# A pair-interaction tower on one core: later units become the moving rows, thirty rounds are added before they are summed

## The reference, cut to what matters

```python
e = jnp.stack([tbl_f[ids[:, f]] for f in range(40)], axis=1)    # 512 x 40 x 64
viW = jnp.einsum('bpd,pde->bpe', e[:, i_idx, :], W)             # all 780 pairs i < j
z = jnp.einsum('bpe,bpe->bp', viW, e[:, j_idx, :])              # 512 x 780
h = jnp.maximum(jnp.concatenate([z, dense_ctx], 1) @ W_top1 + b_top1, 0.0)
h = jnp.maximum(h @ W_top2 + b_top2, 0.0)
y = h @ W_top3
```

## Time and profile before

| | |
|---|---|
| median of 3 runs | 315.83 us (315.57 to 318.13) |
| profiled execution | 316.28 us, of which 314.0 us are the span of its instructions |
| PE busy | 307.4 us (98%) |
| DVE busy | 255.2 us (81%) |
| ACT busy | 135.6 us (43%) |
| POOL busy | 193.2 us (62%) |

### The profile page before, as it was taken

One profiled execution on the slowest core, in us unless ns is written; L12 is line 12 of the kernel. 1 busy time (PEld: TensorE's weight loads), 2 busy tenths in 40 slices (PEclk: granted clock), 3 DMA queues, 4 the chain that ended last, 5 costly groups with the idle time before them and its releaser, 6 DMA issues.

```text
span 314.0 us, 4400 instructions
## 1 busy us (share of the span) xinstructions
PE 307.4 (98%) x1676; PEld 112.0 (36%) x1676; DVE 255.2 (81%) x262; ACT 135.6 (43%) x338; POOL 193.2 (62%) x156
## 2 busy tenths in 40 slices
PE   7999999999999999999999999999999999999996
PEld 2444233333333323333333333333333333333464
DVE  4992999889898888989989999999999999950000
ACT  0497874875539545659974602066000000001032
POOL 3887777777777777777733887746665555650000
PEclk9999999999999999999999999999999999999999
DMA  5936232323223743232325689886779664440000
GB/s 147 316 113 206 66 92 62 93 61 79 74 62 94 277 149 91 58 92 64 92 54 118 142 192 179 166 191 153 167 167 188 139 135 92 94 83 8 10 0 0
DMA packets 16188, 35.87 MB, mean 114 GB/s; under 512 B 3748, under 2 KB 4776, under 8 KB 14504
## 3 DMA queue, kind: packets, MB, share of 16 engines
q0 software_dynamic: 5824, 16.79, 27.6%
q1 hardware_dynamic: 8264, 14.20, 15.1%
q10 hardware_dynamic: 2080, 4.61, 4.2%
HBM read 22.87 MB, written 0.00 MB: 73 GB/s over the span
## 4 chain that ended last, share of the span: by engine, by line
PE 63%; POOL 24%; issue 8%; DMA 3%; DVE 0%; ACT 0%; ACTq 0%
PE y_ps L671 39%; POOL gathered L338 24%; PE z_ps L695 14%; PE y_ps L705 5%; PE t_ps L705 2%; DMA gathered<-in_tbl,ids_sb 2%; PE y_ps L759 2%; DMA ids_sb<-ids_rows 1%; PE t_ps L759 1%; DVE prod L559 0%; PE y_ps L768 0%; ACT prod L472 0%; ACTq L368 0%; ACT y_out L475 0%; DVE x_fold L527 0%
## 5 line engine op out<-in xcount | busy, mean ns | idle before, releaser
L671 PE MATMUL y_ps<-x,w 64*128 64x512 f32 x780 | 182.8, 604 | 0.9 <-DVE prod L559 0.8
L338 POOL DMA_INDIRECT gathered<-in_tbl,ids_sb x128 | 127.6, 997 | 43.4 <-issue 38.4
L559 DVE TENSOR_TENSOR prod<-y_ps,x 128x1024 f32<-128x1024 f32 x89 | 103.8, 1210 | 15.3 <-PE y_ps L671 14.4
L559 DVE TENSOR_TENSOR prod<-y_ps,x_quad 128x1024 f32<-128x1024 f32 x96 | 110.4, 1214 | 1.3 <-issue 0.6
L671 PEld LDWEIGHTS y_ps<-x,w 64*128 64x128 f32 x780 | 70.2, 186 | 113.4 <-issue 81.3
L410 ACT COPY x<-x_fold 32x128 f32<-32x128 f32 x240 | 70.9, 295 | 68.4 <-DVE x_fold L527 65.7
L363 POOL TENSOR_TENSOR prod<-prod 128x2048 f32<-128x2048 f32 x12 | 54.5, 4540 | 33.2 <-DVE prod L559 33.2
L695 PE MATMUL z_ps<-prod,select 128*32 128x512 f32 x588 | 73.4, 600 | 0.0
L439 ACT COPY zT<-z_ps 128x512 f32<-128x512 f32 x6 | 3.5, 586 | 69.7 <-PE z_ps L695 69.7
L695 PEld LDWEIGHTS z_ps<-prod,select 128*32 128x32 f32 x588 | 14.3, 108 | 52.0 <-issue 36.8
L433 ACT COPY x_mix<-x 64x512 f32<-64x512 f32 x40 | 24.7, 617 | 0.7
(11 more groups left out here) (46 smaller groups left out, 89.1 us busy)
## 6 DMA issues: line engine op xcount, KB each, us to landing
w<-w_rows SPq DMA_DIRECT2D x48, 256.0 KB, 2.8
prod<-prod POOLq DMA_DIRECT2D x12, 1024.0 KB, 7.7
gathered<-in_tbl,ids_sb POOLq DMA_INDIRECT x128, 2.5
w<-w_rows ACTq DMA_DIRECT2D x1, 1792.0 KB, 8.2
prod<-in_tbl ACTq DMA_DIRECT2D x6, 256.0 KB, 7.8
prod<-hot_ids SPq DMA_DIRECT2D x4, 256.0 KB, 6.7
prod<-in_tbl ACTq DMA_DIRECT2D x4, 128.0 KB, 3.0
w<-w_rows ACTq DMA_DIRECT2D x1, 512.0 KB, 9.8
```

Source lines behind the costliest of these rows:

```text
L338: nc.gpsimd.indirect_dma_start(gathered[:, slot, c, s * DIM:(s + 1) * DIM], None, tables[f][:, :], bass.IndirectOffsetOnAxis(ap=ids_sb[:, ...
L559: nc.vector.tensor_tensor(prod[:, d % PROD_SLOTS, :, :], y_ps[:, d % DUO_SLOTS, :, :], factor, ALU.mult).then_inc(prod_ready, 1)
L671: last = nc.tensor.matmul(y_ps[:, d % DUO_SLOTS, half, :], w[rows, r % W_SLOTS, d % ROUND, :], x[rows, units[half], :], start=True, stop=True)
```

## The change

`PAIRED` falls from 14 to 10. Units 10 to 19 become moving rows against columns that are regrouped halves of the older units: `("low", u, c)` takes unit u of `x` against the four fields of units 2c and 2c+1. `x_quad` therefore holds units 0 to 17, four copies each, at the duos of `QUAD_AT`. There are now 35 quad rounds, 11 to 15, 17 to 29 and 31 to 47, and 30 of them are added beforehand: odd ones from 11 to 45 by DMA, and 24, 26, 28, 32, 34, 36, 38, 40, 42, 44, 46, 47 by POOL. Rounds 12, 14, 16, 18, 20, 22 and 30 are still summed directly, as are 0 to 10 and 48. TensorE sums round r-1 up to round 11, does no sum in round 12, one block of layer 1 in round 13, and sums round r-3 from round 14 on. The layer-1 block that left the loop goes behind the last round's duos.

`x` has 12 slots, reused; gather slots fall from 6 to 4, weight slots from 8 to 6. POOL issues 65 gathers first and the other 63 behind additions. Unit 11 is turned by TensorE at duo 50. Duos 0 and 1 run ahead of the last part of unit 3's pick; ScalarE makes one of unit 3's one-hots instead of three (VectorE makes the other two) and copies six of the eight `x_mix` pieces and unit 0's `x_quad` ahead of unit 3. The layer-1 weights come in seven DMAs of 256 KB behind rounds 3 to 9.

```diff
-LAYER1_AT = [25, 26]
-GATHER_SLOTS = 6
-W_SLOTS = 8
-PAIRED = 14
-QUADS = (UNITS - PAIRED) // 2
+NO_SUMS_AT = [12, 13]
+GATHER_SLOTS = 4
+X_SLOTS = 12
+DUOS_AHEAD = 2
+W1_LOADED_AT = 3
+W_SLOTS = 6
+PAIRED = 10
+QUADS = UNITS // 2 - 1
...
-FOLD_AT = {5: (4, 7), 6: (8, 12), 7: (16, 19), 8: (22, 26), 9: (29, 32), 10: (36, 40), 11: (43, 47), 12: (50, 54), 13: (58, 62),
-           14: (66, 70), 15: (74, 78), 16: (82, 86), 17: (90, 94), 18: (100, 104), 19: (116, 132)}
-GATHERED_FIRST = 120
-GATHERS_BEHIND = {24: 2, 26: 2, 28: 2, 30: 2}
-ADDED_BY_DMA = [24, 26, 28, 30, 32, 34, 36, 38, 40, 42, 44, 46]
-ADDED_BY_POOL = [25, 27, 29, 31, 33, 35, 37, 39, 41, 43, 45, 47]
+FOLD_AT = {5: (4, 7), 6: (8, 12), 7: (16, 19), 8: (22, 26), 9: (29, 33), 10: (36, 40), 12: (53, 57), 13: (63, 68),
+           14: (72, 77), 15: (86, 100), 16: (109, 118), 17: (127, 133), 18: (141, 151), 19: (161, 169)}
+PE_TRANSPOSES_AT = {11: 50}
+QUAD_AT = {0: 0, 1: 0, 2: 12, 3: 26, 4: 29, 5: 33, 6: 36, 7: 40, 8: 44, 9: 46, 10: 52, 11: 53,
+           12: 57, 13: 68, 14: 77, 15: 100, 16: 118, 17: 133}
+MIX_AT = {0: 0, 4: 19, 8: 52, 12: 100, 16: 169}
+GATHERED_FIRST = 65
+GATHERS_BEHIND = {11: 7, 13: 7, 15: 7, 17: 7, 19: 7, 21: 7, 23: 3, 25: 2, 27: 2, 29: 7, 31: 2, 33: 2, 35: 3}
+ADDED_BY_DMA = [11, 13, 15, 17, 19, 21, 23, 25, 27, 29, 31, 33, 35, 37, 39, 41, 43, 45]
+ADDED_BY_POOL = [24, 26, 28, 32, 34, 36, 38, 40, 42, 44, 46, 47]
...
-MADE_BY_ACT = {2: (5, 6, 7), 3: (5, 6, 7)}
+MADE_BY_ACT = {2: (5, 6, 7), 3: (7,)}
...
+        self.rounds = [pairs[i:i + ROUND] for i in range(0, len(pairs), ROUND)]
+        self.quads_of([10, 11])
+        self.rounds.append(later + self.mixed(11)[1:])
+        self.quads_of([12, 13])
+        self.quads_of([14, 15])
+        self.rounds.append(self.mixed(11)[:1] + self.mixed(15))
+        self.quads_of([16, 17])
+        self.quads_of([18, 19])
+        self.rounds.append(self.mixed(19))
...
+    def quads_of(self, units):
+
+        items = [(u, c) for u in units for c in range(u // 2)]
+        for (u, c), (v, e) in zip(items[::2], items[1::2]):
+            self.rounds.append([("low", u, c), ("low", v, e), ("high", u, c), ("high", v, e)])
...
-        if r < LAYER1_AT[0]:
+        if r < NO_SUMS_AT[0]:
             return r - EARLY_LAG if r >= EARLY_LAG else None
-        return None if r in LAYER1_AT else r - LAG
+        return None if r in NO_SUMS_AT else r - LAG
...
             def save_half(u, s):
+                if s == 0 and u >= X_SLOTS:
+
+                    act.wait_ge(prod_ready, plan.last_row(u - X_SLOTS) + 1)
                 act.wait_ge(unit_folded, 2 * list(FOLD_AT).index(u) + s + 1)
...
+                    if d == 0:
+                        for u in range(HOT_UNITS - 1):
                             save_x(u)
+                        begin_mixture(0)
+                        copy_quad(0)
+                        save_x(HOT_UNITS - 1)
+                        end_mixture(0)
+                        save_x(HOT_UNITS)
+                    for u in FOLD_AT:
+                        for s in range(2):
+                            if FOLD_AT[u][s] == d:
+                                save_half(u, s)
...
+                    for k in MIX_AT:
+                        if MIX_AT[k] == d and k:
+                            begin_mixture(k)
+                            end_mixture(k)
+                    for u in QUAD_AT:
+                        if QUAD_AT[u] == d and u:
+                            copy_quad(u)
+                if W1_LOADED_AT <= r < W1_LOADED_AT + NBLK:
+                    b = r - W1_LOADED_AT
+                    act.dma_start(w1[:, b, :], w1_in[:, b, :]).then_inc(w1_loaded, 16)
...
+                    for d in range(DUOS_AHEAD):
+                        interact(d)
+
                     transpose_unit(HOT_UNITS)
...
             pe.wait_ge(z_saved, NBLK - 2)
-            layer1(0, full[len(LAYER1_AT):-1])
+            layer1(0, full[1:-1])
```

More of the change, by code:

```diff
@@ L80, in __init__ @@
         for u in range(PAIRED):
-            pairs += [("pair", k, u) for k in range(u - u % 2)]
+            own = [("pair", k, u) for k in range(u - u % 2)]
+            later = own[-2:] if u == PAIRED - 1 else []
+            pairs += own[:len(own) - len(later)]
             if u % 4 == 3:
                 pairs += self.mixed(u)
[L84 to L99, removed]
+        self.rounds = [pairs[i:i + ROUND] for i in range(0, len(pairs), ROUND)]
[7 more added lines that the diff above has]
+        self.rounds.append(self.mixed(19))
         assert all(len(r) == ROUND for r in self.rounds[:-1])
@@ L118, in sums_at, with last_row @@
     def sums_at(self, r):
-        if r < LAYER1_AT[0]:
+        if r < NO_SUMS_AT[0]:
             return r - EARLY_LAG if r >= EARLY_LAG else None
-        return None if r in LAYER1_AT else r - LAG
+        return None if r in NO_SUMS_AT else r - LAG
     def is_quad(self, r):
         return self.rounds[r][0][0] == "low"
[L127 to L131, removed]
+    def last_row(self, u):
+        return max(d for d, (kind, k, c) in enumerate(self.duos)
+                   if u == k or kind == "pair" and u == c or kind.startswith("mix") and k <= u < k + 4)
     def transposed_at(self, u):
@@ L139, in transposed_at @@
             return FOLD_AT[u][0]
-        return next(d for d, duo in enumerate(self.duos) if u in duo[1:])
+        return PE_TRANSPOSES_AT[u]
     def tile_pairs(self, d, half):
@@ L413, in save_half, with copy_quad, mix_columns, begin_mixture @@
                     last.then_inc(x_ready, 1)
[L414 to L418, removed]
-                            n = 2 * (u % 2) + s
-                            last = nc.scalar.copy(x_quad[n * QUAD:(n + 1) * QUAD, u - PAIRED - u % 2 + h, :],
-                                                  x[s * DIM + h * QUAD:s * DIM + (h + 1) * QUAD, u, :])
-                    last.then_inc(quad_ready, 1)
-            def save_mixture(k):
+            def copy_quad(u):
+                act.wait_ge(x_ready, u + 1)
+                for s in range(2):
+                    for h in range(2):
+                        n = 2 * (u % 2) + s
+                        last = nc.scalar.copy(x_quad[n * QUAD:(n + 1) * QUAD, u - u % 2 + h, :],
+                                              x[s * DIM + h * QUAD:s * DIM + (h + 1) * QUAD, u % X_SLOTS, :])
+                last.then_inc(quad_ready, 1)
+            def mix_columns(k, units):
+                for n, kind in enumerate(("mix1", "mix2")):
+                    for half, (_, columns) in enumerate(plan.mixture(kind, k)):
+                        for side, (unit, field) in enumerate(columns):
+                            if unit in units:
+                                copied = nc.scalar.copy(x_mix[side * DIM:(side + 1) * DIM, 2 * n + half, :],
+                                                        x[field * DIM:(field + 1) * DIM, unit % X_SLOTS, :])
+                return copied
+            def begin_mixture(k):
                 if k:
@@ L428, in save_mixture, with end_mixture @@
                     act.wait_ge(prod_ready, before + 1)
+                act.wait_ge(x_ready, k + 3)
+                mix_columns(k, (k, k + 1, k + 2))
+            def end_mixture(k):
                 act.wait_ge(x_ready, k + 4)
[L430 to L435 removed]
+                mix_columns(k, (k + 3,)).then_inc(mix_ready, 1)
             def save_z(b):
@@ L671, in interact @@
                     last = nc.tensor.matmul(y_ps[:, d % DUO_SLOTS, half, :], w[rows, r % W_SLOTS, d % ROUND, :],
-                                            x[rows, units[half], :], start=True, stop=True)
+                                            x[rows, units[half] % X_SLOTS, :], start=True, stop=True)
                 last.then_inc(y_ready, 1)
```

53 lines of the change are left out of this document (22 added, 31 removed).

## The result

The changed kernel takes 325.8 us (median of 4 runs), the kernel before 315.7 on the same chip: ratio 1.0289 [1.0226, 1.0352], 2.9% slower. 320.5 was forecast, with 323.5 as the upper end. The profiled execution took 324.59, its span 322.3 against 314.0, so 8.3 of span are to be explained by the two traces.

A forecast was written before the change was run, and what follows sets the result against it. TensorE was taken to bound the kernel, with VectorE level in added rounds. -0.6 - 5.2 + 0.9 + 7.2 + 2.4 = +4.7 on the profiled 316.28 gave 321.0, or 320.5 for the median; range 313 to 323.5.

The forecast's parts named there:

- the hold: Gathers behind a 1 MB addition land 8.1 after its issue; four folds wait 8.0 together, net loss 7.2.
- the wait in period 9: Round 9's duos with the sum that follows; the prediction named no wait there.
- Opening: Two duos run before unit 3's pick ends; duo 2's product at 32.6 instead of 33.2: gain 0.6, between 0 and 1.
- The upper bound: Gathers behind an addition land 8.6 after its issue, net loss 8.8 instead of 7.2.
- Fold at duo 77: Unit 14's second half; its last gather stands second behind round 17's addition: wait 2.2.
- The clock's rival: TensorE stands still about 4.7 at duo 68, restarts at 1.2 GHz; half a period there costs 2.5: 323; chance 0.13.
- Periods 12 to 19: Rounds of duos, each with the sum that follows; forecast 15.3 (12 to 14), 10.2 (15 and 16), 21.2 (17 to 19).
- the 0.8 that the forecast gave back: Direct sums of periods 17 and 19 go on while VectorE waits: about 0.8 off waits of 8.0.
- Halved sums and the old halt: Periods 12 to 47: six sums halved, 6 x 0.85, and a 1.35 halt gone, less folds at 0.28: gain 5.2.
- The `z_saved` copy: Period 43: TensorE waits for ScalarE's block copy behind eight x_mix copies; 2.4 lost, bounds 1.5 and 2.6.
- Layer 1: The block that left the loop stands behind the last duos, hidden by nothing: 0.9 more.
- the forecast without hold and without the copy's wait: Rival: gathers land 2.5 after their own issue, no fold waits, nor TensorE for `z_saved`: 310.9; chance a third of 0.15.

The follow-up runs named there:

- the last two builds: Changed kernel with later folds of units 12 to 14 and last x_mix copies at duo 173: 312.73; plus unit 10's first half folded at duo 38: 310.85.
- The best build: Changed kernel with later folds of units 12 to 14, last x_mix copies at duo 173, unit 10's first half folded at duo 38: 310.85, ratio 0.9836.

## Why the prediction fell short, point by point

The direction was right, and so were most of the places; the sum was +4.7, the two profiled executions differ by 8.3 and the medians by 10.1. Two steps failed. The larger is the hold: a gather behind an addition was taken to land 8.1 after it wherever it stands in line, and rounds 12 to 20 took 51.2 instead of 46.7. The other is the wait in period 9, which the sum has at nothing without a reason.

- **Opening** (-0.6): -0.94 up to round 2, inside its bounds.
- **Period 9** (nothing was forecast): +0.72 in the profiled execution, 0.9 to 2.1 in the profiles of the seven experiments that kept the fold there, 1.9 between the medians of the last two builds that differ by it (312.73 and 310.85). This step failed outright. The forecast let TensorE and VectorE gain 0.6 in the opening and never asked whether the folds of units 5 to 10, whose gathers come at POOL's own unchanged pace, had that much margin. The trace of before showed how little there was: 1.25 at duo 36, less the gain, with landings of up to 3.4. The margin alone would still have sufficed; the slower landing (3.9 instead of 2.48) made the wait, and its cause is open.
- **The hold in POOL's queue** (8.1 for every gather behind an addition): that gathers behind an addition wait for it was right, shown by the packets and by the one gather moved; that POOL's queue does it, and not the DMA engines which the addition takes up, is not shown. The size was right only for the first gather behind it, 8.28; the second takes 9.2, the third 9.27 (10.6 in the execution with the copy moved) and the fourth 9.5 to 9.6. The 8.1 counted the addition's landing, 7.7 before and 8.0 now in the median, and left out the gathers and the weight load that are worked off behind it. The upper bound was also added up wrongly: with 8.6 each of the four waits is 0.5 longer, which makes 9.2 and not 8.8. The waits were 2.77, 1.67 and 4.06 instead of 1.8, 0.1 and 3.9: 8.5 where 5.8 stood.
- **Fold at duo 77** (2.2): no wait. It was taken up by the lower clock behind duo 68, and is 2.93 or 2.87 where the clock stays up there. The clock's rival had the fall right, and nearly its size (2.6 where 2.5 stood), but added it to a wait that it hides. What the Trainium skill says there (TensorE: Matmul & The Clock Gate, Why this matters for your kernels), that a gap between bursts puts the engine back at the lower clock, the trace bears out for the pause of 4.11; behind the pause of 2.4 in period 43 the clock stayed up in this kernel and fell in the one with later folds.
- **Periods 12 to 19** by the table: 51.2 instead of 46.7, or 4.5 more. 2.7 of it are the three waits, and 0.4 is the clock's 2.6 in place of the 2.2 at duo 77. Another 0.85 has nothing to do with waits: without them the forecast's terms for these periods add up to 39.5, and the four kernels whose folds don't wait there take 40.3. The last 0.5 lies within the 0.8 that the forecast gave back for direct sums that go on while VectorE waits; no run splits it off.
- **Halved sums and the old halt** (-5.2): right. With folds that don't wait, rounds 12 to 20 take 40.33, and the additions are worth 5.3 to 5.6. The folds in added periods cost 0.10 to 0.12 each, not 0.28, which is why periods 20 to 47 came out 1.0 under the forecast.
- **The `z_saved` copy** (+2.4): 2.39, in period 43, with the rows of copies in the order and at nearly the times worked out. Taking it away gave 2.7.
- **Layer 1** (+0.9): +0.86, 40.13 against 39.27.

The rest, from the profiled 324.59 to the median of 325.8, is 1.2. No trace shows it; the other kernels' profiles have longer halts in periods 2, 5 and 9 than this one, and these can carry it, but this is argued and not shown. The best build checks the sum from the other side: the forecast without hold and without the copy's wait was 310.9, and the kernel whose folds and copy are moved out of their way takes 310.85. That it fits so closely is in part luck: there too rounds 12 to 20 take 0.85 more than their terms and periods 20 to 47 take 1.0 less.

## What to carry to other kernels

A large DMA issued ahead of small ones delays the first of them by about its own duration, and those behind it by more (here 8.3 and 9.2 to 9.6): count the position in the line behind it, not only the transfer ahead. A step that speeds up the consumer must be held against every producer that keeps its own pace, also far ahead of the change. And when one halt follows another closely, price them together: what the first one costs beyond its place is only what the second would not have taken anyway.

## What the runs showed of the hardware that was not expected

- A gather that stands second to fourth behind a 1 MB accumulating DMA is there 9.2 to 9.6 after the DMA's issue (10.6 once), one that stands first 8.3, although the third one's own issue went out 5.4 before (99.21, used at 104.57), where one alone lands after 2.5.
- The first ten to twelve gathers are issued at an uneven pace, 0.94 to 3.64 busy each, and their sum shifts POOL's whole stream by up to 3.1 from one execution to another (the 46th gather starts at 67.70 in the changed kernel, at 69.41 in the one with the copy moved and at 70.78 in the one with unit 10's fold moved alone).
- Much the same pause of TensorE kept the full clock in one execution and lost it in another. In period 43 a pause of 2.4 left it at 1.00 in the changed kernel and was followed by 0.80 from 250 to 256 with later folds, and by 0.50 from 259 to 262 with the early additions undone (periods 43 and 44 took 7.71 and 5.76). At duo 53 a pause of 2.23 left it at 1.00 from 104 to 110 in the changed kernel, and one of 2.20 in the kernel with one gather moved was followed by 0.51, the third column from the end in the line below. The pause of 4.11 was followed by 0.52, and with matmuls of zeros in it by 1.00. Why the pauses of 2.2 to 2.4 differ stays open.

```profile
107.00:110.00 3.00, 3.00 (x8) 1.15 (x8) 3.00 (x4) 2.92 (x8) 0.82 (x1) 0.51 0.02 5
```
